# Where the causal mask of a decay matrix is written: on GpSimd behind the exponential, or on TensorE under it

## The reference

```python
log_f_cum = cumsum(log_sigmoid(fg))                      # over the tokens, with a leading 0
log_fg = where(tril, log_f_cum[s] - log_f_cum[t], -inf)  # decay from token t to token s, causal
log_D = log_fg + ig[t]
D = exp(log_D - max(log_D, over t))
C = (q @ k.T) / sqrt(16) * D
h = C / (max(|sum(C)|, exp(-max_log_D)) + eps) @ v
```

## Time and profile before

| what | us |
|---|---|
| median of 3 runs | 253.47 |
| the three runs | 253.7, 250.07, 253.47 |
| the profiled execution, whole | 250.66 |
| its span, first to last instruction | 248.8 |
| TensorE matmuls busy | 205.4 (83%) |
| VectorE busy | 142.4 (57%) |
| GpSimd busy | 106.1 (43%) |
| ScalarE busy | 93.0 (37%) |

### The profile page before, as it was taken

How to read it: one execution, slowest core, us unless ns; L and a number is a source line. 1 busy time by engine, 2 the same in 40 slices (tenths; PEclk the granted TensorE clock), 3 DMA queues, 4 the chain that set the end, 5 groups by cost and what they waited for, 6 DMA issues and landing times.

```text
span 248.8 us, 4136 instructions
## 1 busy us (share of the span) xinstructions
PE 205.4 (83%) x1294; PEld 147.4 (59%) x1295; DVE 142.4 (57%) x316; ACT 93.0 (37%) x178; POOL 106.1 (43%) x102
## 2 busy tenths in 40 slices
PE   8393968999958768327799999999999999999950
PEld 3172833444423544213588888888888888888840
DVE  4389297599996957887868777322333223322220
ACT  0550325665553383400366575322323223232310
POOL 7056008888562400005106564465544654455222
PEclk9979899999997858755899999999999999999997
DMA  5959999900020112201102233222432233332321
GB/s 143 253 192 322 378 370 377 362 35 1 3 77 8 44 43 86 86 0 54 30 3 42 45 55 67 49 43 42 66 63 42 42 46 59 59 46 42 31 34 21
DMA packets 20031, 23.40 MB, mean 94 GB/s; under 512 B 3888, under 2 KB 15152, under 8 KB 20016
## 3 DMA queue, kind: packets, MB, share of 16 engines
q1 hardware_dynamic: 12640, 15.89, 19.0%
q0 software_dynamic: 4464, 6.16, 15.5%
q10 hardware_dynamic: 2912, 1.15, 1.7%
HBM read 17.95 MB, written 5.24 MB: 93 GB/s over the span
## 4 chain that ended last, share of the span: by engine, by line
PE 64%; DVE 19%; DMA 5%; ACT 4%; issue 3%; ACTq 2%; POOL 1%; DVEq 0%; POOLq 0%
PE bank L1251 26%; PE bank L1268 15%; PE bank L1082 4%; PE bank L1260 4%; DMA wg_sb<-in_L_xattn_Wf_dram 3%; PE bank L1006 3%; PE bank L1119 2%; DVE arena L720 2%; PE bank L1233 2%; PE bank L1143 2%; DMA out_dram<-hraw,sidx 2%; PE bank L1098 1%; DVE xn_sb L806 1%; PE bank L1052 1%; ACTq L446 1%
## 5 line engine op out<-in xcount | busy, mean ns | idle before, releaser
L436 POOL DMA_INDIRECT out_dram<-hraw,sidx x23 | 37.6, 1637 | 63.3 <-DVE hraw L966 60.3
L1251 PE MATMUL bank<-arena_r,xn_sb_r 128*128 x184 | 57.2, 392 | 0.0
L960 DVE TENSOR_TENSOR x_sb<-x_sb,bank 128x512 f32<-128x512 f32 x23 | 15.8, 688 | 57.3 <-ACT x_sb L594 57.3
L1268 PE MATMUL bank<-w_sb,xn_sb 128*128 x184 | 43.6, 380 | 0.8 <-ACT xn_sb L598 0.8
L1251 PEld LDWEIGHTS bank<-arena_r,xn_sb_r 128*128 128x128 f32 x184 | 34.8, 189 | 7.1
L1251 PE MATMUL bank<-w_sb_r,xn_sb_r 128*128 x92 | 38.4, 417 | 0.4 <-DVE w_sb_r L858 0.4
L1268 PEld LDWEIGHTS bank<-w_sb,xn_sb 128*128 128x128 f32 x184 | 33.2, 190 | 4.6 <-issue 1.0
L594 ACT ACTIVATE x_sb<-bank 128x512 f32<-128x512 f32 x23 | 13.7, 597 | 49.4 <-PE bank L1251 49.4
L390 POOL TENSOR_SCALAR_AFFINE_SELECT arena<-arena 128x1024 f32<-128x1024 f32 x16 | 18.1, 1134 | 25.9 <-ACT arena L494 25.8
L419 POOL DMA_INDIRECT cvT<-xnorm_scratch,gidx x12 | 12.0, 1004 | 29.3 <-DVE gidx L918 26.0
L598 ACT ACTIVATE xn_sb<-bank 128x512 f32<-128x512 f32 x23 | 13.8, 598 | 25.8 <-PE bank L1260 25.8
(11 more groups left out here) (183 smaller groups left out, 270.6 us busy)
## 6 DMA issues: line engine op xcount, KB each, us to landing
w_sb<-in_L_ffn_w_dram SPq DMA_DIRECT2D x24, 512.0 KB, 9.1
x_sb<-in_x_dram SPq DMA_DIRECT2D x2, 512.0 KB, 7.3
arena<-in_ctx_dram ACTq DMA_DIRECT2D x2, 512.0 KB, 10.7
xnorm_scratch<-xn_sb SPq DMA_DIRECT2D x8, 128.0 KB, 1.8
out_dram<-x_sb SPq DMA_DIRECT2D x8, 128.0 KB, 1.8
out_dram<-hraw,sidx POOLq DMA_INDIRECT x23, 3.8
cvT<-xnorm_scratch,gidx POOLq DMA_INDIRECT x12, 2.9
hc<-xnorm_scratch,gidx POOLq DMA_INDIRECT x11, 2.8
```

The costliest lines, as they stand in the source:

```text
L436: nc.gpsimd.indirect_dma_start(out=out[:, :], out_offset=bass.IndirectOffsetOnAxis(ap=sidx[:, i:i + 1], axis=0), in_=y_sb[i % 2], in_offse ...
L960: nc.vector.tensor_tensor(h_sb[p], sg_sb[p], ps_scores[p][:, 1, :], ALU.mult).then_inc(s_hm, 1)
L1251: last = nc.tensor.matmul(ps_scores[p][:, n, :], a, w, start=(k == 0 and j == 0), stop=(k == KC - 1 and j == 2))
L1268: last = nc.tensor.matmul(ps_tr[:, 0:H], hT_sb[p][:, k * P:(k + 1) * P], w2_sb[:, bass.ds(e * W2 + k * H, H)], start=(k == 0), stop=(k == ...
```

## The change

A matrix future (bf16) is made that holds -1e30 where s < t and 0 elsewhere, together with an identity matrix in bf16. In each call of differences() two matmuls of 512 columns write identity x future into both banks of ps_diff, once for each of four heads, and the matmuls that were there add onto it. The exponential of -1e30 is 0, so GpSimd's select behind it is left out, and c_mult waits for the exponential (s_ex) instead of for the select (s_dm). On GpSimd's queue mask_q of the later sequences and add_heads thereby follow each other directly. Four instructions that make the two constants stand near the beginning of GpSimd's queue, ahead of those that make the head blocks.

```diff
+        ident_b = sb("ident_b", [P, P], BF16)
+        future = sb("future", [P, P], BF16)
...
+            nc.gpsimd.memset(ident_b[:], 0.0).then_inc(s_fut, 1)
+            nc.gpsimd.memset(future[:], 0.0).then_inc(s_fut, 1)
+            pool.wait_ge(s_fut, 2)
+            nc.gpsimd.affine_select(out=ident_b[:], in_=ident_b[:], compare_op=ALU.not_equal, fill=1.0, base=0,
+                                    pattern=[[-1, P]], channel_multiplier=1).then_inc(s_fut, 1)
+            nc.gpsimd.affine_select(out=future[:], in_=future[:], compare_op=ALU.is_ge, fill=-BIG, base=0,
+                                    pattern=[[1, P]], channel_multiplier=-1).then_inc(s_fut, 1)
...
-            def mask_decay(n):
-                pool.wait_ge(s_ex, n + 1)
-                d = dec[:, n % 4]
-                nc.gpsimd.affine_select(out=d, in_=d, compare_op=ALU.is_ge, fill=0.0, base=0,
-                                        pattern=[[0, HC], [1, S]], channel_multiplier=-1).then_inc(s_dm, 1)
...
             for b in range(B):
-                mask_decay(2 * b)
-                mask_decay(2 * b + 1)
                 if b + EARLY < B:
                     mask_q(b + EARLY)
...
-                dve.wait_ge(s_dm, n + 1)
+                dve.wait_ge(s_ex, n + 1)
...
                 if n == 0:
                     pe.wait_ge(s_msk, 2)
+                    pe.wait_ge(s_fut, 4)
...
+                for c in range(KC):
+                    nc.tensor.matmul(ps_diff[:, c, :], ident_b[:], future[:, :].unsqueeze(1).to_broadcast([P, 4, S]),
+                                     start=True, stop=False)
                 for c, r in enumerate(rows):
                     nc.tensor.matmul(ps_diff[:, c, :], ax_r[r, a, :],
                                      sel_r[r, 4 * b:4 * b + 4].unsqueeze(2).to_broadcast([64, 4, S]),
-                                     start=True, stop=False, tile_position=(c * 64, 0))
+                                     start=False, stop=False, tile_position=(c * 64, 0))
```

More of the change, by code:

```diff
@@ L247, in bass_gated_mlstm_moe_kernel @@
         s_sq = sem("heads_squared")
+        s_fut = sem("future_masked")
         s_dm = sem("decay_masked")
```

## The result

The changed kernel takes 256.41 us (median of 4 runs, 255.99 to 256.6), the kernel before 252.16 (median of 4, 250.07 to 253.7). The ratio of the comparison is 1.022, with a 95% interval from 1.018 to 1.027: slower, while whether by more than 2% the interval leaves open. The comparisons leave disturbed executions out, which the medians keep. The four times of the kernel before also lie apart (250.07 and 250.85 us, 253.47 and 253.7), so the ratio is not the quotient of the medians, 1.017. The forecast was 257.5 us and 1.6% slower, the range 252.5 to 261.5. The profiled execution takes 256.6 us, its span is 254.7 against 248.8.

A forecast was written before the change was run, and what follows sets the result against it. TensorE was taken to bound the stage throughout: held logf +1.4 us, three first calls +1.80, six pairs of 6.03, clock -1.3, last call +0.6 put the last c_mult +4.0; 253.5 + 4.0 = 257.5 us, range 252.5 to 261.5.

The forecast's parts named there:

- TensorE is the bound throughout: Stage up to scores(14): TensorE gets there at 79.1 us, VectorE alone would at 72.7, so TensorE sets the time.
- The price of a call: Each of 16 calls of differences(): two new matmuls 0.43 us plus 0.17 for the shape change, 0.60 us.
- The part that no row of before showed: Change of the array's shape around the new matmuls in each call: 0.17 us, taken between 0.11 and 0.21.
- The pair: Two half steps in the stage: 5.06 us plus 0.60 and 0.37 for their calls, 6.03 us.
- The cover by ScalarE's copy: Second half step's call: transposition waits for ScalarE's copy anyway, hiding 0.23 us, so the call adds 0.37 us.
- The three calls ahead of scores(2): Start of the stage: three calls all on the path, +1.80 us.
- What moved unasked: GpSimd's mask_q(4) to mask_q(7), no longer behind fills, run from 25.5 to 32.9 us and hold VectorE's logf.
- The end of logf: VectorE's logf L730, held by a GpSimd multiplication, ends near 33.0 us instead of 31.6: +1.4 us for all behind it.
- the sum: Stage: +4.8 us at scores(14), 6.6 us from there to the last c_mult, which ends at 85.7 us, +4.0.
- The relief of VectorE: Stage without GpSimd's fills, TensorE as before: last c_mult 3.0 us earlier, but not collected since TensorE isn't free.
- the fall near 75 us: TensorE's lower clock from 74 to 80 us, which cost about 1.3 us before, should not occur: -1.3 us.
- rival (a): Calls dearer, +6.3 us at 0.75 us each, near 2 more if idle behind logf lowers the clock: 260 to 262; chance 0.33.

The follow-up runs named there:

- hold_q: Changed kernel with GpSimd's last four multiplications (mask_q) each waiting again for the exponential that stood ahead of them before; 253.8 us, 1.009 to the kernel before.
- no_mask_hold: Changed kernel without new matmuls or fills (no mask, exponential with scale 0), GpSimd's last four multiplications held back; 247.37 us, 0.986 to the kernel before.
- double: Changed kernel with the two new matmuls of each call issued a second time, added on; 263.5 us, 1.038 to the kernel before.
- rows64: Changed kernel with new matmuls over 64 rows each, one per bank, half the mask left out, exponential with scale 0; 249.62 us, 0.994 to the kernel before.
- mix_even: Kernel before with TensorE writing the mask in half steps 4, 6, 8, 10, 12 and 14, GpSimd filling the others; 249.02 us, ratio 0.986.
- mix3: Kernel before with TensorE writing the mask in half steps 10, 12 and 14 alone, GpSimd filling the other thirteen; 247.94 us, ratio 0.985.
- warm: Changed kernel with twelve extra matmuls filling TensorE's waits, eight behind center_v(3) and four behind scores(0); 254.42 us, 1.009 to the kernel before.
- early_q: Kernel before, fills kept on GpSimd, with all eight multiplications of the queries ahead of the loop (EARLY 8 instead of 4); 251.67 us, ratio 1.000.
- no_mask: Changed kernel without the two new matmuls of a call and without fills, exponential with scale 0; 248.29 us, 0.983 to the kernel before.
- mix8: Kernel before with TensorE writing the mask in half steps 8 to 15, GpSimd filling in 0 to 7; 251.69 us, ratio 0.995.
- mix_odd: Kernel before with TensorE writing the mask in half steps 5, 7, 9, 11, 13 and 15, GpSimd filling the others; 249.05 us, ratio 0.987.
- hold_warm: Changed kernel with GpSimd's last four multiplications held back and twelve matmuls filling TensorE's waits; 254.11 us, 1.007 to the kernel before.

## Why the prediction was right, point by point

**The bound.** "TensorE is the bound throughout" held: a busy share of 1.00 from 65 to 80 us, and removing the calls gives back some 7 of the 8.5 us that they take (hold_q against no_mask_hold).

**The price of a call.** 0.60 us was forecast, with bounds of 0.43 and 0.75; the trace has 0.53, and double splits it into 0.43 of streaming and 0.10 for the change of shape and the load of ident_b. The part that no row of before showed was taken as 0.17. It is the low neighbour, 0.11 (scores behind another shape), that it resembled, not the middle. The Trainium skill's rule (TensorEngine Tiling (Array Packing), Key Properties), that a change of mode drains the engine, agrees in sign with the 0.10 us. rows64, where no further change is needed, pays 0.11 us for everything, but its two matmuls also run over different rows side by side, so it doesn't price the change by itself.

**The pair.** Forecast 6.03 us, measured 6.00 in the chain and 5.98 on the mean of six. The cover by ScalarE's copy was sized well: covered calls add 0.39 to 0.40 us (mix_even 5.45, mix3 66.14 - 60.68 = 5.46), uncovered ones 0.54. The three calls ahead of scores(2) were put at 1.80 us and cost 1.6 (hold_q has scores(2) 1.82 us later than the kernel before, and logf 0.19).

**What moved unasked.** The block of multiplications was forecast at 25.5 to 32.9 us and lies at 25.51 to 32.96. logf takes 1.25 us instead of 0.29, not the 1.7 forecast, but only because it starts 0.5 us later (31.85 instead of 31.33). TensorE's clock was low from 21.7 to 28.5 us there, where before it was low from 23.9 to 27.4. The end of logf is set by GpSimd and is what the sum used: forecast 1.4 us later, measured 33.10 against 31.62, 1.5 us later. In warm logf starts at 31.21 and ends at 33.09 all the same. hold_q shows that the move is a cause and not an accompaniment.

**The relief of VectorE.** 3.0 us were worked out for a kernel without fills and with TensorE as before; no_mask_hold has scores(14) 3.5 us earlier (70.86 against 74.33), and the last product 5.0, the further 1.6 us where the clock fell at 75 us before and doesn't now. So 3.5 against 3.0. That it isn't collected in the changed kernel was right.

**The clock.** Forecast: the fall near 75 us goes, 1.3 us; right (scores(14) to the last product 6.33 us, forecast 6.6). Not in the sum: a fall behind the held logf, which I had put into rival (a) at near 2 us. It is there, 2.5 us by warm, and it is the term that the sum lacked: the sum had scores(2) at 42.9, warm, without the fall, has 42.76, the changed kernel 45.23.

So the forecast time came out close partly by luck. In the profiled executions the last product is 5.74 us later, where the sum said 4.0. The 1.7 us between them are 2.5 us of clock that were left out, less some 0.7 us by which the calls and the end of the stage were taken too long (0.1 us up to scores(2), 0.3 in the six pairs, 0.3 behind them). What hid the gap is the base: the forecast started from a median of 253.47 us, and with a fourth run that median is 252.16. Added to the profiled execution of 250.66 us, the 4.0 us would have given 254.7, and it is 256.6. In the medians the difference is 4.25 us; the ratio of the comparison says 2.2%. The chance for slower by over 2%, 0.37, was if anything small, because the fall of the clock was treated as a companion of dear calls instead of a case of its own.

## What to carry to other kernels

When an instruction is taken off an in-order queue, look at what stood behind it: it now runs as early as its own waits allow, and if it holds up another engine there (here logf on VectorE, 1.25 us instead of 0.29 beside a multiplication on GpSimd), it can land on the chain. Ask for each part of a stage which engine bounds it before moving work between engines: the same move was worth 1.5% in the three half steps where the receiving engine had room, and cost 0.9% when made in all sixteen with GpSimd's multiplications kept in place, 2.2% with them moved. A wait on TensorE costs its own length and, if the clock falls behind it, more: scores(1) took 2.08 us at the lower clock, where scores take 1.02 at the full one. Twelve cheap matmuls in the waits were worth 2.5 us up to scores(2).

## What was not expected of the hardware

TensorE's clock does not follow from the program alone. With logf held and nothing in the wait it fell between 34 and 43 us in three profiled executions (changed, early_q, double) and not in a fourth (no_mask); with nothing held it stayed up in six (before, hold_q, mix3, mix8, mix_odd, no_mask_hold) and fell in two (rows64, with logf at 0.35 us, 33.5 to 40.4 us, and mix_even, 34.7 to 44.9). The stretches of mix_even there, with logf at its 0.29 us and no wait of TensorE longer than 1.07 us between 29 and 35 us:

```profile
34.00:40.00 6.00, 5.05 (x18) 2.07 (x16) 4.42 (x13) 1.58 (x3) 1.09 (x1) 0.56 1.07 375
40.00:45.00 5.00, 3.88 (x24) 1.52 (x24) 2.75 (x4) 2.25 (x3) 3.28 (x3) 0.51 1.07 371
```

With filled waits it stayed up in both (warm, hold_warm). That the waits make the fall likelier fits all of this, and so do the times of warm and hold_q, ten runs each, and the mean clocks of their runs. It is not shown how often the clock falls in each kernel. The clock also goes with the spread between runs of one kernel: in 76 of the 77 runs of the kernel before beside the experiments (the other took 350.12 us), the 21 with a mean clock of 0.906 or less have a median of 253.75 us, the 18 with 0.917 or more one of 250.8. Where in those runs it fell is not on record. Second, a pair of 64-row matmuls ahead of another of the same shape costs 0.11 us for 512 columns, less than the 0.21 us that 512 columns take from one matmul to the next in the earlier trace rows.
